# Attention layer: scores moved to the head of each head pair, attention to its tail

## Chip, cores and metric

The program runs on one core of one Trainium2 chip. The metric is device time in microseconds (us), the median of several runs of the whole program. All times of instructions come from one profiled execution.

## The reference

A conditioned transformer layer on x of 16 batches x 256 tokens x 256 features, float32, with 16 heads of 64, and 8 experts:

```python
shift = silu(t) @ W_ada.T + b_ada
h = _ln(x, ln1_g, ln1_b) + shift
qkv = (h @ Wqkv.T).reshape(b, n, 3, H, HD)
q = _ln(q, qn_g, qn_b); k = _ln(k, kn_g, kn_b)           # per head
attn = softmax(einsum('bhnd,bhmd->bhnm', q, k) / sqrt(HD))
x = x + (attn @ v).reshape(...) @ Wout.T
gate = softmax(tok @ Wgate.T); top_k per expert (512 tokens each)
tok += w * (gelu(_ln(tok[idx]) @ fc1.T + b1) @ fc2.T + b2)   # scattered back
```

## The kernel before

Stage 1 (to about 890 us) is the attention half and the gate products; stages 2 and 3 are the routing and the experts. Only stage 1 is touched.

Stage 1 is a software pipeline over batches `b` (-1 to 16; a hardware loop for 2 to 13, the rest written out) and, in a batch, over 8 **pairs** of heads, `hp` 0 to 7, unit `u = 8b + hp`. Every engine has a function `batch` that walks the pairs in the same order, each with its own instruction stream, executed strictly in the order written; semaphores (`need`) join the streams. In pair `u`:

- TensorE (PE) transposes the probabilities of unit u-2 into `mx` (L1634) and the normalised q and k of unit u+1 into `pq` (L1643); makes the scores of unit u into `sc` (`scores`, L1590); multiplies the transposed probabilities of u-2 with V into `av` (L1689, the "attention"); and does one or two **chunks** of the q, k, v projection into a bank of `ch` (`chunk`, lines L508 to L510, two chunks of 6 matmuls in pairs 7, 0, 1, 3, 4, 5). In pair 2 the output projection of pairs 4 to 7 of the batch before takes the chunks' place, in pair 6 that of pairs 0 to 3, with transposes of `tok` and the gate products (L1705). At the end of pair 1 the next batch's input rows are transposed (`xh`, L1607).
- ScalarE (ACT) brings q out of `pq` (L1186), the chunks out of `ch` (`raw` and `sq`, or `V`), makes `qk_hi` (L1152), the four exponentials (L1170, in two halves of two, `exponentials(u, hp, 0)` and `(u, hp, TT)`), and `o_hi` from `av` (L1224). In pairs 1 and 5 it starts the square-root iteration for the norms (`power_guess`, L1094 and L1096).
- VectorE (DVE) copies `mx` to `probT` (L1419), brings k out (L1427), sums squares (L1360), makes `var` (L1373, L1376), takes the row extremum `m` of the scores (L1470), `o_lo` from `av` and `o_hi` (L1479), the reciprocals (L1398).
- GpSimd (POOL) normalises the probabilities of u-1 (L1059), in pairs 1 and 5 refines the reciprocal roots (`refine`, L1018 to L1028) and scales a quarter of q/k (L965), and at the end of every pair makes `qk_lo` of unit u+1 (L1076).

Large products are exact-split: `_hi` and `_lo` operands in fp32r, three matmuls each. Transposes, attention and gate products are plain f32. The shape of a matmul in the array differs too: the scores use half its rows (64 x 128, two side by side), the attention half its columns (128 x 64, two side by side), all others the whole of it (128 x 128).

Scores of unit u wait for two counters:

```python
need(lo_ready, u + 1)     # qk_lo of this unit, from POOL in pair u-1
need(prob_ready, u)       # exponentials of unit u-1 have read sc
```

In the order of before, PE goes: `mx`, `pq`, first chunk, attention, scores, second chunk.

Of the kernel before, what the change touches and what calls it, by code (L numbers as in the profile page):

```python
# [80 lines left out]
def make_counts():  # L81
# [8 lines left out]
    for b in range(-1, B + 1):  # L90
        cur, nxt, prv = 0 <= b < B, b + 1 < B, 1 <= b <= B
        for hp, pos, name, who in batch_slots(b):
            key = (hp, pos)
            hit("slot", b, key)
            hit(who, b, key)
            if name == "gate":
                slots[-1] = (b, (6, 0), who, key)
            else:
                slots.append((b, key, who, key))
            if name in ("q", "k"):  # L100
                hit("chunk", b, key)
# [93 lines left out]
def build(nc, x, condT, w_adaT, vecs, w_qk, w_vT, w_outT, w_gateT, experts, b2s, consts, out):  # L195
    ctx = ExitStack()
    with ctx:
# [887 lines left out]
        def _(act):  # L1085
# [58 lines left out]
            def batch(b, cur, nxt, prv):  # L1144
# [15 lines left out]
                def exponentials(u, hp, first):  # L1160
# [11 lines left out]
                    if first > 0:  # L1172
                        ins.then_inc(prob_ready, 1)

                for hp in range(UNITS):
                    u = b * UNITS + hp
                    par = (hp + 1) % 2
                    ahead = (cur and nxt) or (cur and hp < UNITS - 1) or (nxt and hp == UNITS - 1)
                    live = (hp, 0) in CHUNKS and (cur if hp < 2 else nxt)
                    if ahead:  # L1180

                        need(qk_transposed, u + 2)
                        need(lo_ready, u)
                        if entry:
                            need(q_vec_ready, 1)
                        nc.scalar.activation(qkT[par][:, 0:N], pq[:, 0:N], ACT.Identity,  # L1186
                                             bias=q_vec[:, 1:2], scale=q_vec[:, 0:1]).then_inc(q_evacuated, 1)
# [28 lines left out]
                    if tail and hp == UNITS - 1:  # L1216
                        exponentials(u, hp, 0)
                    if (cur and hp > 1) or (hp < 2 and prv):
                        need(attended, u - 1)
                        if hp == 2 and prv:  # L1220
                            need(slot_filled, through("slot", b - 1, (6, 2)))
                        if hp == 6 and prv:
                            need(slot_filled, through("slot", b, (2, 0)))
                        nc.scalar.activation(o_hi[:, (hp - 2) % UNITS, :], av[:, 0:N], ACT.Copy).then_inc(o_hi_ready, 1)  # L1224
                    if live and values:
                        chunk(b, hp, 0)
# [4 lines left out]
                    if hp == 5 and nxt and not entry:  # L1231
                        power_guess(b, 4)
                    if live and values:
                        chunk(b, hp, 1)
                    if cur and not (tail and hp == UNITS - 1):
                        exponentials(u, hp, 0)
                    if cur:
                        exponentials(u, hp, TT)
                    if tail and hp == 5:
                        power_guess(b, 4)  # L1240
# [6 lines left out]
        def _(dve):  # L1247
# [155 lines left out]
            def batch(b, cur, nxt, prv):  # L1403
                last_entry = isinstance(b, int) and b == B
                entry = isinstance(b, int) and b < 0
                for hp in range(UNITS):
                    u = b * UNITS + hp
                    if entry and hp == 2:
                        silu_of_condition()
# [63 lines left out]
                    if hp == 2 and nxt and not entry:  # L1473
                        split_rows(b)
                    if (cur and hp > 1) or (hp < 2 and prv):

                        need(o_hi_ready, u - 1)
                        pair = (hp - 2) % UNITS
                        nc.vector.tensor_tensor(o_lo[:, pair, :], av[:, 0:N], o_hi[:, pair, :].bitcast(F32), ALU.subtract).then_inc(o_split, 1)  # L1479
                    if hp in (0, 3, 4, 7) and (cur if hp < 2 else nxt):  # L1480
# [29 lines left out]
                    if isinstance(b, int) and b == 0 and hp == 0:  # L1510
                        split_wout(2)

            per = 5
# [13 lines left out]
        def _(pe):  # L1527
# [75 lines left out]
            def transposed(bank, rows):  # L1603
# [4 lines left out]
                ins.then_inc(slot_filled, 1)  # L1608

            def batch(b, cur, nxt, prv):  # L1610
                drain = isinstance(b, int) and b == B
                for hp in range(UNITS):
# [23 lines left out]
                    if ahead:  # L1636
# [29 lines left out]
                    if hp == 6 and cur:  # L1666
# [4 lines left out]
                        project(first, (0, 1), False)  # L1671
                    filled = nxt or hp < 3
                    if cur and not filled:
                        scores(u, hp % 2)
                    if behind:

                        need(probT_ready, u - 1)
                        if drain:
                            need(probT_other_ready, hp + 1)
                        need(o_split, u - 2)  # L1680
                        i = (hp - 2) % GU
                        gpar = ((hp - 2) // GU) % 2
                        if i == 0:

                            need(act_read, through("act", b, (1, 1)) if hp == 6 else through("act", b, (0, 0)) - 1)
                        for jt in range(TT):
                            for hh in range(2):
                                at = (hh * TT + jt) * N
                                ins = nc.tensor.matmul(av[hh * HD:(hh + 1) * HD, 0:N], V[gpar][:, jt, i * P + hh * HD:i * P + (hh + 1) * HD],  # L1689
                                                       probT[:, at:at + N], start=(jt == 0), stop=(jt == TT - 1))  # L1690
                        ins.then_inc(attended, 1)
                    if cur and filled:
                        scores(u, hp % 2)
                    if live:
                        chunk(b, hp, 1)
                    if hp == 1 and nxt:
                        bank = take_bank(b, (1, 2))
                        need(xh_ready, b + 2)
                        transposed(bank, xh)
                    if hp == 6 and prv:  # L1700
                        bank = ch[slot_bank(b, (6, 1))]
# [5 lines left out]
                        ins.then_inc(slot_filled, 1)  # L1707
                    if hp == 2 and prv:
                        need(o_split, u - 2)
                        project(second, (7,) if drain else (6, 7), True)  # L1710
                    if hp == 6 and cur:
                        need(o_split, u - 2)
                        project(first, (2, 3), True)

# [48 lines left out]
```

## Time and profile before

| | us |
|---|---|
| median of 3 runs | 1157.24 (1156.55 to 1157.64) |
| time of the profiled execution | 1159.4 |
| its span, first to last instruction | 1157.6 |
| TensorE matmul busy | 1101.2 (95%) |
| VectorE busy | 899.9 (78%) |
| ScalarE busy | 731.6 (63%) |
| GpSimd busy | 607.3 (52%) |

Busy time of matmuls overlaps (they are pipelined), so the starts of successive groups say more than the busy column. One batch of the loop lasts 53.5 us. Times below are from the start of the span; a merged line gives the start of its first instruction, the time to the end of its last, and their count; in brackets the idle time before and what ended it.

### The profile page before, as it was taken

To read this page: it belongs to the slowest core of one execution; us is meant where nothing else is said; L and a number is where in the kernel's file an instruction comes from. 1 tells how busy PE (TensorE), PEld (TensorE's weight loads), DVE (VectorE), ACT (ScalarE), POOL (GpSimd) and SP (SyncE) were. 2 spreads that over 40 slices of the span, in tenths; PEclk is the share of its full clock that TensorE was granted. 3 is DMA by queue.
4 is the path that set the end of the run, shared out by engine and by line. 5 is a ranking of instruction groups with operands and counts; after the bars stand their busy time and mean duration, and the time that the engine had idled before them with its cause. 6 is when DMAs were issued, how large, how long until landed. Compare 5 with 4: busy or idle time off the path is not lost.

```text
span 1157.6 us, 24504 instructions
## 1 busy us (share of the span) xinstructions
PE 1101.2 (95%) x8046; PEld 860.9 (74%) x8052; DVE 899.9 (78%) x1693; ACT 731.6 (63%) x1991; POOL 607.3 (52%) x529
## 2 busy tenths in 40 slices
PE   8899999999999999999999999999988779999996
PEld 6667777777777777777777777777765248889985
DVE  6897888878887878788787878787776867777773
ACT  5667777776767677777777676777773214455441
POOL 2556555666666556656565665656562023554332
PEclk9899999999999999999999999999999998999999
DMA  5000000000000000000000000000002404554422
GB/s 184 17 10 19 20 20 19 18 18 18 18 18 20 27 25 18 18 18 18 18 18 18 18 18 18 30 15 20 10 19 84 132 18 132 168 134 119 109 29 28
DMA packets 31776, 48.62 MB, mean 42 GB/s; under 512 B 7921, under 2 KB 28529, under 8 KB 30449
## 3 DMA queue, kind: packets, MB, share of 16 engines
q1 hardware_dynamic: 25584, 39.49, 10.5%
q0 software_dynamic: 6144, 8.52, 4.0%
q8 instruction: 28, 0.46, 0.2%
q14 instruction: 20, 0.16, 0.0%
HBM read 35.29 MB, written 12.71 MB: 41 GB/s over the span
## 4 chain that ended last, share of the span: by engine, by line
issue 31%; PE 31%; POOL 21%; DVE 8%; ACT 6%; POOLq 1%; DMA 1%; SPq 0%; ACTq 0%; DVEq 0%
POOL qk_lo L1076 9%; POOL prob L1059 5%; PE ch L508 5%; PE ch L510 4%; PE ch L509 4%; POOL qn L965 3%; PE av L1689 3%; DVE m L1470 2%; PE sc L1590 2%; ACT prob L1170 2%; ACT raw L1125 1%; PE sc L508 1%; PE sc L510 1%; PE sc L509 1%; PE pq L1643 1%
## 5 line engine op out<-in xcount | busy, mean ns | idle before, releaser
L1059 POOL TENSOR_TENSOR prob<-prob,inverse 128x1024 f32<-128x1024 f32 x127 | 241.1, 1899 | 265.4 <-DVE inverse L1398 265.4
L1170 ACT ACTIVATE prob<-sc,m 128x256 f32<-128x256 f32 x512 | 235.9, 475 | 121.3 <-DVE m L1470 118.2
L1470 DVE TENSOR_REDUCE m<-sc 128x4 f32<-128x1024 f32 x127 | 155.4, 1224 | 69.9 <-PE sc L1590 69.7
L1419 DVE COPY probT<-mx 128x1024 f32<-128x1024 f32 (+1 forms) x128 | 155.2, 1212 | 59.2 <-PE mx L1634 58.1
L1076 POOL TENSOR_TENSOR qk_lo<-qkT,qk_hi 128x512 fp32r<-128x512 f32 x128 | 171.5, 1340 | 26.0 <-ACT qk_hi L1152 24.5
L508 PE MATMUL ch<-w_hi,hT_lo 128*128 128x512 f32 x384 | 170.1, 443 | 2.6 <-DVE hT_lo L1332 2.2
L509 PE MATMUL ch<-w_lo,hT_hi 128*128 128x512 f32 x384 | 152.3, 397 | 0.0
L510 PE MATMUL ch<-w_hi,hT_hi 128*128 128x512 f32 x384 | 152.0, 396 | 0.0
L1689 PE MATMUL av<-probT,V 128*64 128x256 f32 x1024 | 139.6, 394 | 8.3 <-DVE probT L1419 3.8
L1634 PE MATMUL mx<-con,prob 128*128 128x128 f32 x1024 | 134.5, 274 | 9.1 <-POOL prob L1059 7.8
L1634 PEld LDWEIGHTS mx<-con,prob 128*128 128x128 f32 x1024 | 116.0, 140 | 29.0 <-POOL prob L1059 11.7
L1689 PEld LDWEIGHTS av<-probT,V 128*64 128x64 f32 x1024 | 62.4, 136 | 69.0 <-DVE probT L1419 38.0
L1170 ACT ACTIVATION_READ_ACCUMULATOR prob<-sc,m 128x1 f32 x512 | 105.4, 206 | 0.0
L612 POOL DMA_INDIRECT out<-yout,index x32 | 52.3, 1634 | 99.9 <-DVE yout L958 93.5
L673 ACT ACTIVATE yT<-ch,b_sb 128x512 f32<-128x512 f32 x62 | 42.7, 689 | 88.5 <-PE ch L510 87.4
L1360 DVE TENSOR_REDUCE ssum<-sq 128x8 f32<-128x512 f32 x128 | 86.7, 678 | 13.2 <-ACT sq L1127 13.1
L1125 ACT ACTIVATE raw<-ch 128x512 f32<-128x512 f32 x128 | 78.0, 609 | 30.0 <-PE ch L510 30.0
L508 PEld LDWEIGHTS ch<-w_hi,hT_lo 128*128 128x128 f32 x384 | 72.3, 188 | 26.8 <-issue 2.2
L1590 PE MATMUL sc<-qk_hi,qk_lo 64*128 64x256 f32 x512 | 85.7, 330 | 1.9 <-ACT prob L1170 1.4
L1590 PEld LDWEIGHTS sc<-qk_hi,qk_lo 64*128 64x128 f32 x512 | 48.3, 184 | 50.5 <-issue 48.8
L510 PEld LDWEIGHTS ch<-w_hi,hT_hi 128*128 128x128 f32 x384 | 72.3, 188 | 17.7
L1186 ACT ACTIVATE qkT<-pq,q_vec 128x256 f32<-128x256 f32 x128 | 73.6, 575 | 18.5 <-PE pq L1643 18.4
(222 smaller groups left out, 2686.9 us busy)
## 6 DMA issues: line engine op xcount, KB each, us to landing
fcw<-experts SPq DMA_DIRECT2D x8, 2048.0 KB, 9.0
x_sb<-x SPq DMA_DIRECT2D x16, 256.0 KB, 2.7
xr_sb<-x SPq DMA_DIRECT2D x16, 256.0 KB, 2.8
out<-tok SPq DMA_DIRECT2D x16, 256.0 KB, 2.2
rows_dram<-xh SPq DMA_DIRECT2D x16, 256.0 KB, 2.2
prob<-w_qk SPq DMA_DIRECT2D x2, 512.0 KB, 6.5
qn<-w_qk SPq DMA_DIRECT2D x2, 512.0 KB, 7.2
V<-w_vT SPq DMA_DIRECT2D x2, 512.0 KB, 7.3
```

What stands on the lines that cost most here:

```text
L508: nc.tensor.matmul(psum, l_lo, r_hi, start=first, stop=False)
L509: nc.tensor.matmul(psum, l_hi, r_lo, start=False, stop=False)
L510: return nc.tensor.matmul(psum, l_hi, r_hi, start=False, stop=last)
L1059: nc.gpsimd.tensor_tensor(pr, pr, r, ALU.mult).then_inc(normalised, 1)
L1076: nc.gpsimd.tensor_tensor(qk_lo[par][:, :], qkT[par][:, :], qk_hi[par][:, :].bitcast(F32), ALU.subtract).then_inc(lo_ready, 1)
L1125: nc.scalar.activation(raw[:, c, :], bank[:, :], ACT.Copy)
L1170: ins = nc.scalar.activation(prob[hp % 2][:, g * N:(g + 1) * N], sc[:, g * N:(g + 1) * N], ACT.Exp, bias=m[hp % 2][:, g:g + 1], scale=-1.0 ...
L1419: nc.vector.tensor_copy(probT[:, 0:half], mx[:, 0:half]).then_inc(probT_ready, 1)
L1470: nc.vector.tensor_reduce(m[hp % 2][:, :], sc[:, :].rearrange("p (g n) -> p g n", n=N), AX.X, ALU.min).then_inc(max_ready, 1)
L1590: ins = nc.tensor.matmul(sc[:, at:at + N], q_part[par][rows, it * P:(it + 1) * P], k_part[par][rows, N:2 * N], start=(q_part is qk_lo), st ...
L1634: ins = nc.tensor.transpose(mx[:, to:to + P], pr[:, at:at + P], ident)
L1689: ins = nc.tensor.matmul(av[hh * HD:(hh + 1) * HD, 0:N], V[gpar][:, jt, i * P + hh * HD:i * P + (hh + 1) * HD], probT[:, at:at + N], start ...
```

## The change

In pairs with scores, `cur and (nxt or hp < 3)`, that is all pairs of batches 0 to 14 and pairs 0 to 2 of batch 15, the PE order becomes: `mx`, `pq`, (in pair 2 the transposes of `xh`, which leave pair 1), **scores**, first chunk, second chunk (in pair 2 both halves of the output projection; in pair 6 the transposes of `tok`, both halves, then the gate products), **attention**. ACT takes `o_hi` from between the chunks' reading and `qk_hi` to between the two halves of the exponentials, and with it, in pairs 1 and 5, the two readings of `V` (one ahead of and one behind the second half). DVE takes `o_lo` to the end of its pair. The counting of filled slots follows the new PE order. No instruction is added or taken away.

```diff
@@ make_counts
+        for hp, pos, name, who in sorted(batch_slots(b), key=lambda s: (s[0], 3 if s[2] == "gate" else s[1])):
+            hit("slot", b, (hp, pos))
         for hp, pos, name, who in batch_slots(b):
             key = (hp, pos)
-            hit("slot", b, key)
             hit(who, b, key)
@@ ACT, pair hp
+                    behind = (cur and hp > 1) or (hp < 2 and prv)
+                    under = cur and (nxt or hp < 3)
...
-                    if (cur and hp > 1) or (hp < 2 and prv):
-                        need(attended, u - 1)
...
-                        nc.scalar.activation(o_hi[:, (hp - 2) % UNITS, :], av[:, 0:N], ACT.Copy).then_inc(o_hi_ready, 1)
-                    if live and values:
+                    if behind and not under:
+                        attended_high(hp, u)
+                    if live and values and not under:
                         chunk(b, hp, 0)
                     if ahead and not (tail and hp > 1):
                         split_high(u, par)
...
                     if cur and not (tail and hp == UNITS - 1):
                         exponentials(u, hp, 0)
+                    if behind and under:
+                        attended_high(hp, u)
+                    if live and values and under:
+                        chunk(b, hp, 0)
                     if cur:
                         exponentials(u, hp, TT)
+                    if live and values and under:
+                        chunk(b, hp, 1)
@@ DVE, end of pair hp
+                    if behind and under:
+                        attended_low(hp, u)
@@ PE, pair hp
                         ins.then_inc(qk_transposed, 1)
+                    if hp == 2 and nxt and cur:
+                        bank = take_bank(b, (1, 2))
+                        need(xh_ready, b + 2)
+                        transposed(bank, xh)
+                    filled = nxt or hp < 3
+                    if cur and filled:
+                        scores(u, hp % 2)
                     if live:
                         chunk(b, hp, 0)
...
-                    if cur and filled:
-                        scores(u, hp % 2)
+                    if behind and not filled:
+                        attend(b, hp, u, drain)
                     if live:
                         chunk(b, hp, 1)
-                    if hp == 1 and nxt:
+                    if hp == 1 and nxt and not cur:
...
+                    if hp == 2 and prv:
+                        need(o_split, u - 2)
+                        project(second, (7,) if drain else (6, 7), True)
+                    if hp == 6 and cur:
+                        need(o_split, u - 2)
+                        project(first, (2, 3), True)
                     if hp == 6 and prv:
                         bank = ch[slot_bank(b, (6, 1))]
...
+                    if behind and filled:
+                        attend(b, hp, u, drain)
```

## Rows read from the trace of the kernel before

**Rows 1.** Page, part 4: shares of the chain of work that ended last.
```profile
issue 31%; PE 31%; POOL 21%; DVE 8%; ACT 6%; POOLq 1%; DMA 1%; SPq 0%; ACTq 0%; DVEq 0%
```

**Rows 2.** Windows, one batch, pair 7 to pair 6: length, busy time (xcount), clock, DMA.
```profile
core 0: us, PE busy (x) PEld busy (x) DVE busy (x) ACT busy (x) POOL busy (x), PEclk, DMA share, GB/s
505.16:558.70 53.54, 52.70 (x394) 40.85 (x393) 43.36 (x75) 38.57 (x116) 32.05 (x29) 1.00 0.07 20
```

**Rows 3.** Timeline, PE, pair 1: start, us, engine, line, operation, out<-in, shapes, count.
```profile
518.21 1.04 PE L1634 MATMUL mx<-con,prob 128*128 128x128 f32 x8
519.08 0.60 PE L1643 MATMUL pq<-con,qn 128*128 128x128 f32 x4
519.44 0.48 PE L508 MATMUL ch<-w_hi,hT_lo 128*128 128x512 f32 x1
...
521.01 1.08 PE L1689 MATMUL av<-probT,V 128*64 128x256 f32 x8
522.03 0.39 PE L1590 MATMUL sc<-qk_hi,qk_lo 64*128 64x256 f32 x2
...
522.93 0.51 PE L508 MATMUL ch<-w_hi,hT_lo 128*128 128x512 f32 x1
523.28 0.39 PE L509 MATMUL ch<-w_lo,hT_hi 128*128 128x512 f32 x1
...
524.44 0.60 PE L1607 MATMUL ch<-con,xh 128*128 128x128 f32 x4
524.87 1.04 PE L1634 MATMUL mx<-con,prob 128*128 128x128 f32 x8
```

**Rows 4.** Timeline, PE, first transposes of pairs 3 and 6.
```profile
531.41 1.09 PE L1634 MATMUL mx<-con,prob 128*128 128x128 f32 x8
...
551.11 1.03 PE L1634 MATMUL mx<-con,prob 128*128 128x128 f32 x8
```

**Rows 5.** Timeline, PE, last batch, end of pair 6 and start of pair 7.
```profile
870.09 1.08 PE L1689 MATMUL av<-probT,V 128*64 128x256 f32 x8
871.11 1.06 PE L1705 MATMUL ch<-wg_sb,tokT 128*128 128x8 f32 x8
...
873.54 1.04 PE L1634 MATMUL mx<-con,prob 128*128 128x128 f32 x8
874.51 0.39 PE L1590 MATMUL sc<-qk_hi,qk_lo 64*128 64x256 f32 x2
```

**Rows 6.** Timeline, ACT, pair 1.
```profile
522.14 0.39 ACT L1224 ACTIVATE o_hi<-av 128x256 fp32r<-128x256 f32 x1 [0.71 <-PE av L1689]
522.43 0.59 ACT L1130 ACTIVATE V<-ch 128x512 f32<-128x512 f32 x1
...
523.42 0.23 ACT L1094 ACTIVATE log_var<-var 128x36 f32<-128x36 f32 x1
```

**Rows 7.** Timeline, ACT, last batch, third exponential to the end of the fourth.
```profile
857.50 0.47 ACT L1170 ACTIVATE prob<-sc,m 128x256 f32<-128x256 f32 x1
...
858.31 0.21 ACT L1170 ACTIVATION_READ_ACCUMULATOR prob<-sc,m 128x1 f32 x1
```

**Rows 8.** Timeline, PE, last batch, the scores that waited for those exponentials.
```profile
858.67 0.39 PE L1590 MATMUL sc<-qk_hi,qk_lo 64*128 64x256 f32 x2 [0.72 <-ACT prob L1170]
```

**Rows 9.** Timeline, POOL, pair 1 and pair 5 (the last rows reach into pair 6).
```profile
520.67 1.90 POOL L1059 TENSOR_TENSOR prob<-prob,inverse 128x1024 f32<-128x1024 f32 x1 [2.44 <-DVE inverse L1398]
...
526.50 1.28 POOL L1076 TENSOR_TENSOR qk_lo<-qkT,qk_hi 128x512 fp32r<-128x512 f32 x1
...
547.80 1.89 POOL L1059 TENSOR_TENSOR prob<-prob,inverse 128x1024 f32<-128x1024 f32 x1 [3.15 <-DVE inverse L1398]
550.68 0.25 POOL L1018 TENSOR_TENSOR na<-guess 128x36 f32<-128x36 f32 x1 [0.98 <-ACT guess L1096]
...
553.42 1.28 POOL L1076 TENSOR_TENSOR qk_lo<-qkT,qk_hi 128x512 fp32r<-128x512 f32 x1
```

**Rows 10.** Timeline, DVE, pair 5.
```profile
548.66 1.06 DVE L1373 TENSOR_SCALAR var<-mv 128x4 f32<-128x4 f32 x1
```

**Rows 11.** Timeline, ACT, pair 5.
```profile
550.10 0.23 ACT L1094 ACTIVATE log_var<-var 128x36 f32<-128x36 f32 x1
```

More of the change, by code:

```diff
@@ L1173, in exponentials, with attended_high @@
                         ins.then_inc(prob_ready, 1)
+                def attended_high(hp, u):
+                    need(attended, u - 1)
+                    if hp == 2 and prv:
+                        need(slot_filled, through("slot", b - 1, (6, 2)))
+                    if hp == 6 and prv:
+                        need(slot_filled, through("slot", b, (2, 0)))
+                    nc.scalar.activation(o_hi[:, (hp - 2) % UNITS, :], av[:, 0:N], ACT.Copy).then_inc(o_hi_ready, 1)
                 for hp in range(UNITS):
@@ L1217, in batch @@
                         exponentials(u, hp, 0)
-                    if (cur and hp > 1) or (hp < 2 and prv):
-                        need(attended, u - 1)
[L1220 to L1223, printed above, removed]
-                        nc.scalar.activation(o_hi[:, (hp - 2) % UNITS, :], av[:, 0:N], ACT.Copy).then_inc(o_hi_ready, 1)
-                    if live and values:
+                    if behind and not under:
+                        attended_high(hp, u)
+                    if live and values and not under:
                         chunk(b, hp, 0)
@@ L1232, in batch @@
                         power_guess(b, 4)
-                    if live and values:
+                    if live and values and not under:
                         chunk(b, hp, 1)
@@ L1405, in batch, with attended_low @@
                 entry = isinstance(b, int) and b < 0
+                def attended_low(hp, u):
+                    need(o_hi_ready, u - 1)
+                    pair = (hp - 2) % UNITS
+                    nc.vector.tensor_tensor(o_lo[:, pair, :], av[:, 0:N], o_hi[:, pair, :].bitcast(F32), ALU.subtract).then_inc(o_split, 1)
                 for hp in range(UNITS):
                     u = b * UNITS + hp
+                    behind = (cur and hp > 1) or (hp < 2 and prv)
+                    under = cur and (nxt or hp < 3)
                     if entry and hp == 2:
@@ L1474, in batch @@
                         split_rows(b)
[L1475 to L1479, printed above, removed]
+                    if behind and not under:
+                        attended_low(hp, u)
                     if hp in (0, 3, 4, 7) and (cur if hp < 2 else nxt):
@@ L1511, in batch @@
                         split_wout(2)
+                    if behind and under:
+                        attended_low(hp, u)
             per = 5
@@ L1608, in transposed, with attend @@
                 ins.then_inc(slot_filled, 1)
+            def attend(b, hp, u, drain):
+                need(probT_ready, u - 1)
+                if drain:
+                    need(probT_other_ready, hp + 1)
+                need(o_split, u - 2)
+                i = (hp - 2) % GU
+                gpar = ((hp - 2) // GU) % 2
+                if i == 0:
+                    need(act_read, through("act", b, (1, 1)) if hp == 6 else through("act", b, (0, 0)) - 1)
+                for jt in range(TT):
+                    for hh in range(2):
+                        at = (hh * TT + jt) * N
+                        ins = nc.tensor.matmul(av[hh * HD:(hh + 1) * HD, 0:N], V[gpar][:, jt, i * P + hh * HD:i * P + (hh + 1) * HD],
+                                               probT[:, at:at + N], start=(jt == 0), stop=(jt == TT - 1))
+                ins.then_inc(attended, 1)
             def batch(b, cur, nxt, prv):
@@ L1671, in batch @@
                         project(first, (0, 1), False)
-                    filled = nxt or hp < 3
                     if cur and not filled:
                         scores(u, hp % 2)
[L1675 to L1691, printed above, removed]
-                    if cur and filled:
-                        scores(u, hp % 2)
+                    if behind and not filled:
+                        attend(b, hp, u, drain)
                     if live:
                         chunk(b, hp, 1)
-                    if hp == 1 and nxt:
+                    if hp == 1 and nxt and not cur:
                         bank = take_bank(b, (1, 2))
@@ L1699, in batch @@
                         transposed(bank, xh)
+                    if hp == 2 and prv:
+                        need(o_split, u - 2)
+                        project(second, (7,) if drain else (6, 7), True)
+                    if hp == 6 and cur:
+                        need(o_split, u - 2)
+                        project(first, (2, 3), True)
                     if hp == 6 and prv:
@@ L1707, in batch @@
                         ins.then_inc(slot_filled, 1)
[L1708 to L1713, printed above, removed]
+                    if behind and filled:
+                        attend(b, hp, u, drain)
             over_batches(pe, batch)
```

## The prediction, made before the changed kernel ran

> **What bounds the kernel now.** I read the chain of waits first, then the busy windows of one batch, then PE's timeline pair by pair, then the other engines' timelines around one place in pairs 1 and 5. The chain [rows 1] gives most of the span to PE and to its issue, a fifth to POOL. One batch, cut at the first transposes of pair 7, lasts 53.54 us with PE busy for 52.70 at a granted clock of 1.00 (2.4 GHz) [rows 2]: in stage 1 PE is nearly always at work, and the clock has nothing to lose or win there. So the change is worth what it does to the starts of PE's groups: the edges between them, and the waits in front of them.
>
> A plain pair, by starts in pair 1 [rows 3]: `mx` 0.87, `pq` 0.36, first chunk 1.57, attention 1.02, scores 0.90, second chunk 1.51, together 6.23 up to 524.44; the transposes of `xh` add 0.43. No wait is in it. The waits of the batch come out by subtraction: pairs 7 and 0 take 518.21 - 505.16 = 13.05 against 2 x 6.23 = 12.46, so 0.59; pairs 3 to 5 take 551.11 - 531.41 = 19.70 against 18.69, so 1.01 [rows 2 to 4]. Pair 2 takes 6.54, and streams as many columns as a plain pair; I give it a wait of 0.2. Together **1.8 us of waiting per batch**, which a better order could remove: mostly `mx` behind POOL's normalising and attention behind the copy of `mx`.
>
> **Part 1, edges on PE.** Joining f32 to f32 work saves only if a change of type costs something. Transposes (f32) to chunk (fp32r): 519.08 to 519.44 is 0.36 for four transposes that cost 0.109 each in `mx` (0.87 / 8), so the chunk starts 0.08 early and its first matmul is late by as much: no cost. Chunk back to transposes: five matmuls from 523.28 to 524.44 are 0.232 each up to the transposes, again none [rows 3]. What does cost is a change of shape. Scores (64 rows) to chunk (128 x 128), both fp32r: the first matmul takes 0.35 (522.93 to 523.28) and not 0.23 [rows 3]. Whole array to scores: in the last batch eight transposes take 0.97 up to the scores, and not 0.87, so 0.10 [rows 5]. Attention to whole array, f32 to f32: 1.02, as long as attention to scores [rows 3, 5], so its tail is no cheaper for meeting its own type.
>
> The new order has one shape change more: whole to scores, scores to whole, whole to attention, attention to whole, where before attention and scores stood together. In starts: `mx` 0.89 (0.02 for the load behind attention, an estimate below the 0.10 edges), `pq` 0.44, edge 0.10, scores 0.90, first chunk 1.51 (it now has the place of 522.93 to 524.44), second chunk 6 x 0.232 + 0.10 = 1.49, attention 1.02: **6.35, or +0.12 a pair**, +0.96 a batch (pairs 2 and 6 have the same edges). Bounds: 0 if the loads hide, 0.3 if the new edges cost as much as scores to chunk does in all. The two rules of the Trainium skill differ here: TensorE: Matmul & The Clock Gate (Step-by-step: what each phase is for) has weight loads pulled ahead of running matmuls, and by that alone the order would cost nothing and the sum be 14 us lower; TensorEngine Tiling (Array Packing) (Key Properties) says a change of tiling mode drains the engine, which speaks against this change. The 0.10 edges agree with the second.
>
> **Part 2, waits that go.** The normalised probabilities and `probT` get more time: POOL's normalising, undelayed in pair 1, ends 2.46 + 1.90 = 4.36 us into the pair [rows 3, 9], and `mx` of it comes at the next pair's start, 6.35; attention comes 5.3 us into its pair, the `probT` copy over 3 us before that. I take all 1.8 away (at the least 1.0). DVE's `o_lo` at the pair's end is due in the next attention but one group later; the projections that read it in pairs 2 and 6 come over 3 us into the pair. No cost, and nothing waits behind it but the next `probT` copy, which needs `mx` anyway (0.87 in).
>
> **Part 3, scores behind the exponentials.** Scores now want to start 0.89 + 0.44 + 0.10 = 1.43 into the pair, where they were at 3.82 [rows 3]. ACT has `o_hi` between its two halves of exponentials, and ACT's queue is in order: the second half waits for the attention, now PE's last group. From the start of attention: `o_hi` at +1.13 (521.01 to 522.14), 0.28 to the next instruction [rows 3, 6], two exponentials 858.31 + 0.21 - 857.50 = 1.02 [rows 7], 0.15 to the scores (858.52 to 858.67) [rows 7, 8]: +2.58, while PE gets from attention to the scores in 1.02 + 1.43 = 2.45. **Wait 0.12 a pair**, for six pairs 0.72 a batch. It is a loop through ACT and PE and no later pair wins it back. Bounds: 0, and 0.4 if ACT itself comes late to `o_hi`.
>
> **Part 4, scores behind `qk_lo`.** In pairs 1 and 5 POOL has refine and scaling ahead of `qk_lo`, and that starts from `var`. In pair 5 the little `var` operation lasts 1.06 us and ends at 549.72 with POOL's normalising (547.80 + 1.89 = 549.69) [rows 9, 10]: it does not run beside it. With no delay of `mx`, normalising ends 4.36 into the pair, as in pair 1 [rows 9]; so the logarithm on ACT starts about 4.55. From there to the end of `qk_lo` it was 553.42 + 1.28 - 550.10 = 4.60 in pair 5, and 526.50 + 1.28 - 523.42 = 4.36 in pair 1 [rows 6, 9, 11]; nothing in it is changed. So `qk_lo` ends 9.15 after pair 5 begins. The pair is 6.47 long, the semaphore takes 0.1 (estimate, under the 0.15 above), so the scores of pair 6 start 2.78 in: **wait 1.35**. For pair 2: 4.5 + 4.36 - 6.47 + 0.1 = 2.5 in, where `xh` brings the wish to 1.43 + 0.44 = 1.87: **wait 0.6**. Before, scores came late enough to cover this; nothing covers it now. In the other pairs POOL makes `qk_lo` straight behind `qk_hi`, long ahead. Bounds: by ACT alone (V's 0.48 between, 522.43 to the next) pair 6 waits at least 0.6, pair 2 at least 0.16; above, 1.8 and 1.0 if POOL is a little later than that.
>
> **Sum.** Per batch +0.96 - 1.80 + 0.72 + 0.60 + 1.35 = **+1.83 us**. Batches 1 to 14 have it whole; batch 0 (no attention in pairs 0 and 1) and the three pairs of batch 15 count as one more: 15 x 1.83 = 27 us. Stages 2 and 3 have nothing of it. The profiled execution, 1159.4, becomes 1186; it stands 2.2 us over the median of the runs, so the median becomes **1184 us**.
>
> **Rivals.**
> A, POOL is in time (chance 0.15): `qk_lo` ends sooner because the logarithm starts as soon as it may and POOL runs freer. Then only ACT holds the scores, 0.72 + 0.16 + 0.60 a batch: 0.96 - 1.80 + 1.48 = +0.64, 15 x = 10 us, 1167. For it: ACT is free earlier in pair 5 than before. Against: the five steps on POOL are the same.
> B, faster (0.11): neither counter is late, the scores go straight behind the transposes. 0.96 - 1.80 = -0.84 a batch, 1144. It decides at `qk_lo` of pair 5 ending under 1.4 into pair 6, 1.3 sooner than I find, and all waits together under 0.84 a batch. For it: DVE starts the row extremum 2.4 us earlier, so ACT's exponentials can too. Against: ACT's order, which ties the second half to attention.
> C, ACT comes late (0.14): first half of the exponentials, behind the chunk's reading and `qk_hi`, is not done when attention is. By my count they end together, without reserve; 0.2 late in six pairs is 1.2 a batch more, 18 us: 1202.
> D, loads hide (0.05): edges cost nothing, +0.87 a batch, 1170. The rows of part 1 are against it.
>
> **How the numbers follow.** Forecast 0.55, 1184, by itself 1174 to 1195. The range reaches to A and D below and C above: 1163 to 1205. A measurement of this kernel tells 0.2%, about 2.3 us, from no change. Faster is B, 0.11; the same needs a mean between B and A, 0.05; slower 0.84.
>
> **What would show it.** In the new trace: scores of pair 6 idle over 1 us with `qk_lo` as releaser, of pair 2 about half of that; 0.1 or so in the other pairs behind the exponentials; no wait of attention for `probT`; first matmul of the scores and of the first chunk slow, second chunk's not; `o_hi` as the last thing ahead of the second half of the exponentials, ACT idle before it in pairs 2 and 6. A batch of 55.4 us. I am wrong if the batch is under 53.5, if the scores of pair 6 start under 2 us into the pair, or if transposes behind attention start 0.1 sooner than the gate products did.

## The result and the profile after

The changed kernel takes **1197.96 us** (median; 1197.0 to 1199.42) against 1156.89 measured beside it: ratio 1.0357 [1.034, 1.0373]. It is slower, as forecast, within the range, 14 us over the point. First come the page's busy times and its chain of work, to be compared with [rows 1], then the window of one batch, pair 7 to pair 6, with the columns of [rows 2].

```profile
PE 1112.4 (93%) x8046; PEld 868.6 (73%) x8052; DVE 897.2 (75%) x1693; ACT 734.6 (61%) x1991; POOL 605.4 (51%) x529
...
PE 36%; issue 31%; POOL 21%; DVE 5%; ACT 4%; DMA 1%; POOLq 1%; SPq 1%; ACTq 0%; DVEq 0%
```

```profile
531.78:587.69 55.91, 53.29 (x395) 41.20 (x393) 43.06 (x75) 38.73 (x115) 31.94 (x29) 1.00 0.06 19
```

The same matmuls now take 55.91 us and not 53.54 [rows 2], at the same clock. The part of the batch in which PE is not busy grew from 0.84 to 2.62 us. This is a plain pair, pair 1, to be compared with [rows 3]:

```profile
488.86 1.09 PE L1673 MATMUL mx<-con,prob 128*128 128x128 f32 x8
489.79 0.60 PE L1682 MATMUL pq<-con,qn 128*128 128x128 f32 x4
490.50 0.39 PE L1611 MATMUL sc<-qk_hi,qk_lo 64*128 64x256 f32 x2
490.69 0.31 PE L1611 MATMUL sc<-qk_lo,qk_hi 64*128 64x256 f32 x2
...
491.40 0.50 PE L509 MATMUL ch<-w_hi,hT_lo 128*128 128x512 f32 x1
491.73 0.40 PE L510 MATMUL ch<-w_lo,hT_hi 128*128 128x512 f32 x1
...
492.90 0.40 PE L509 MATMUL ch<-w_hi,hT_lo 128*128 128x512 f32 x1
493.13 0.39 PE L510 MATMUL ch<-w_lo,hT_hi 128*128 128x512 f32 x1
...
494.39 1.08 PE L1645 MATMUL av<-probT,V 128*64 128x256 f32 x8
495.40 1.09 PE L1673 MATMUL mx<-con,prob 128*128 128x128 f32 x8
```

By the starts alone, `mx` takes 0.93, `pq` 0.71 with a wait at its end, the scores 0.90, the chunks 1.50 and 1.49, the attention 1.01. The scores of pairs 2, 3 and 6 (one line each) wait longer, and for POOL:

```profile
497.84 0.39 PE L1611 MATMUL sc<-qk_hi,qk_lo 64*128 64x256 f32 x2 [0.47 <-POOL qk_lo L1077]
...
505.00 0.39 PE L1611 MATMUL sc<-qk_hi,qk_lo 64*128 64x256 f32 x2 [0.65 <-POOL qk_lo L1077]
...
525.60 0.39 PE L1611 MATMUL sc<-qk_hi,qk_lo 64*128 64x256 f32 x2 [1.14 <-POOL qk_lo L1077]
```

Pairs 7, 0, 1, ... 6, from `mx` to `mx`, last 6.54, 6.47, 6.54, 7.42, 7.08, 6.47, 6.53, 8.85 us; before the change they lasted 6.76, 6.29, 6.67, 6.54, 6.83, 6.44, 6.44, 7.63 (the transposes of `xh`, 0.43, went from pair 1 to pair 2). By span, 39.9 us were added: 0.5 ahead of batch 0, 5.4 in its pairs 0 to 6, 4.2 from its pair 7 to pair 6 of batch 1, 30.5 in the 13 batches behind that (2.35 each), 0.9 from there to the end of stage 1; stages 2 and 3 gave 1.6 back.

### The profile page after: what moved, and what is told of

Read it like the earlier page. It is cut to its first block, busy times and chain, and to the rows that moved or that the text cites. A ratio compares the mean times of both kernels' runs of the same rounds, so it can differ in the third digit from the quotient of the medians.

```text
span 1197.5 us, 24532 instructions
## 1 busy us (share of the span) xinstructions
PE 1112.4 (93%) x8046; PEld 868.6 (73%) x8052; DVE 897.2 (75%) x1693; ACT 734.6 (61%) x1991; POOL 605.4 (51%) x529
## 4 chain that ended last, share of the span: by engine, by line
PE 36%; issue 31%; POOL 21%; DVE 5%; ACT 4%; DMA 1%; POOLq 1%; SPq 1%; ACTq 0%; DVEq 0%
POOL qk_lo L1077 9%; PE ch L509 6%; PE ch L511 5%; PE ch L510 5%; POOL prob L1060 5%; PE sc L1611 3%; POOL qn L966 3%; PE mx L1673 3%; PE av L1645 2%; PE sc L509 1%; PE sc L510 1%; PE sc L511 1%; DVE hit L846 1%; ACT sq L1128 1%; PE pq L1682 1%
## 5 line engine op out<-in xcount | busy, mean ns | idle before, releaser
L1171 ACT ACTIVATE prob<-sc,m 128x256 f32<-128x256 f32 x512 | 238.8, 479 | 62.6 <-DVE m L1492 55.5
L509 PE MATMUL ch<-w_hi,hT_lo 128*128 128x512 f32 x384 | 163.9, 427 | 0.8 <-DVE hT_lo L1345 0.8
L1673 PEld LDWEIGHTS mx<-con,prob 128*128 128x128 f32 x1024 | 109.8, 141 | 52.5 <-issue 45.0
L1673 PE MATMUL mx<-con,prob 128*128 128x128 f32 x1024 | 139.8, 279 | 3.5 <-POOL prob L1060 3.4
L1424 DVE TENSOR_TENSOR o_lo<-av,o_hi 128x256 fp32r<-128x256 f32 x128 | 54.1, 423 | 88.0 <-ACT o_hi L1183 85.4
L1611 PEld LDWEIGHTS sc<-qk_hi,qk_lo 64*128 64x128 f32 x512 | 52.9, 185 | 74.7 <-POOL qk_lo L1077 46.9
L509 PEld LDWEIGHTS ch<-w_hi,hT_lo 128*128 128x128 f32 x384 | 73.3, 191 | 27.4 <-DVE hT_lo L1345 1.0
```

Of the source, the lines that this page charges most:

```text
L509: nc.tensor.matmul(psum, l_lo, r_hi, start=first, stop=False)
L1171: ins = nc.scalar.activation(prob[hp % 2][:, g * N:(g + 1) * N], sc[:, g * N:(g + 1) * N], ACT.Exp, bias=m[hp % 2][:, g:g + 1], scale=-1.0 ...
L1611: ins = nc.tensor.matmul(sc[:, at:at + N], q_part[par][rows, it * P:(it + 1) * P], k_part[par][rows, N:2 * N], start=(q_part is qk_lo), st ...
L1673: ins = nc.tensor.transpose(mx[:, to:to + P], pr[:, at:at + P], ident)
```

## The experiments

All started from the changed kernel and kept its arithmetic. The pair's lengths below are from `mx` to `mx` in the steady loop, "+2.87" is a start counted from the pair's `mx`.

**e1: scores back between the chunks**, attention at the tail.

```diff
@@ PE, pair hp
-                    if cur and filled:          # behind pq and xh
-                        scores(u, hp % 2)
                     if live:
                         chunk(b, hp, 0)
...
-                    if cur and not filled:
+                    if cur:                     # between the chunks
                         scores(u, hp % 2)
```

> The changed kernel with one thing moved: scores stand between the two chunks (in pairs 2 and 6 between the two halves of the output projection), attention stays at the tail. Theory (the loss is waits in front of the scores, for qk_lo in pairs 2, 3 and 6 and for the exponentials elsewhere, plus 0.12 us a pair of shape changes): the scores start 2.9 us or later into the pair, all these waits go, the four shape changes stay; a plain pair 6.35, a batch 52.7 to 53.0 us, 1142 to 1148 in all, under the kernel before. Rival (attention at the tail is what costs, through the late o_hi and o_lo): a batch stays above 55, 1185 to 1198.

Measured 1173.19 us, ratio 1.0127 [1.0103, 1.0151]. Plain pairs are all 6.39 with the scores at +2.87: their waits are gone. But pair 2 grew to 7.63 and pair 6 is still 8.50, for a wait that neither the prediction nor the expectation names: the output projection waits for a bank that ACT frees too late, with its second reading of `V`, which the change had moved behind the exponentials. First the line of the table of waits (us in total, times, longest), then the row of pair 6:

```profile
PE ch L509 <- ACT V L1131: 15.5, 29, 0.9
```

```profile
454.74 0.38 PE L509 MATMUL ch<-wo_hi,o_lo 128*128 128x256 f32 x1 [0.56 <-ACT V L1131]
```

Some 25 of the 41 us hang on the place of the scores. The time expected, 1142 to 1148, was missed by 25; the bank is 11 of these (e5).

**e2: scores at the tail**, directly ahead of the attention.

```diff
@@ PE, pair hp
-                    if cur and filled:          # behind pq and xh
-                        scores(u, hp % 2)
...
+                    if cur and filled:          # behind both chunks
+                        scores(u, hp % 2)
                     if behind and filled:
                         attend(b, hp, u, drain)
```

> Scores moved further, directly ahead of the attention at the tail, so that the two narrow shapes stand together again. Theory: one shape change less than with scores between the chunks; a plain pair 6.23, a batch 51.8 us, 1127 to 1133 in all. Rival (shape changes are hidden by loads pulled ahead, and only waits count): the same as with the scores between the chunks, within 3 us. Second rival (row extremum and exponentials now come too late and hold POOL's normalising and the transposes): slower than with scores between the chunks.

Measured 1329.77, ratio 1.1477 [1.1449, 1.1505]; pairs of 7.54 to 9.36. The theory fell. Its second rival was right that the row extremum and the exponentials come too late, but not in what they hold: the transposes are not delayed. In the plain pairs it is the second chunk that waits, 1.1 us, as ACT's readings of the chunks stand behind the exponentials. From the table of waits:

```profile
ACT prob L1171 <- DVE m L1492: 361.9, 124, 5.2
...
PE ch L509 <- ACT sq L1128: 71.2, 62, 2.7
```

**e3: attention back between the chunks**, scores early.

```diff
@@ PE, pair hp
-                    if behind and not filled:   # between the chunks
+                    if behind:
                         attend(b, hp, u, drain)
...
-                    if behind and filled:       # at the tail
-                        attend(b, hp, u, drain)
```

> Scores stay directly behind the transposes, attention goes back between the chunks. Theory: the loop attention, o_hi, second half of the exponentials, next scores is cut, so the 0.13 us in front of the scores of plain pairs goes and a plain pair is 6.35; the waits for qk_lo in pairs 2, 3 and 6 stay or grow a little, as POOL's work counts from the start of its pair. A batch 55.0 to 55.4, 1183 to 1190 in all. Rival (qk_lo alone is the cost): 1197 to 1199, unchanged. Rival (joining attention to the transposes did save something on PE): slower than 1198.

Measured 1195.88, ratio 1.0327 [1.0304, 1.0351]. The loop through ACT is gone: in pair 0 the scores come at +1.45, where in the changed kernel they come at +1.56.

```profile
422.85 1.09 PE L1673 MATMUL mx<-con,prob 128*128 128x128 f32 x8
423.77 0.60 PE L1682 MATMUL pq<-con,qn 128*128 128x128 f32 x4
424.30 0.39 PE L1611 MATMUL sc<-qk_hi,qk_lo 64*128 64x256 f32 x2
```

The pair is 6.47 all the same: now both chunks stand behind another shape, and each has a slow first matmul, where in the changed kernel the transposes behind the attention lose 0.06 in all (0.93 against 0.87; in e3 they take 0.87 in pairs 1 to 6, though 0.92 in the pair shown). Attention ahead of the transposes is the cheaper place, by about the 0.1 that the loop costs. The range expected was missed by 6 us.

**e4: POOL makes `qk_lo` first** in pairs 1 and 5, ahead of refinement and scaling.

```diff
@@ POOL, pair hp
+                    early = hp in (1, 5) and cur and nxt
+                    if early:
+                        ...                     # qk_lo of unit u + 1
                     if hp == 1 and cur:
                         refine(b, 0)
                         scale(b, 0, 2)
```

> The changed kernel with one thing moved on POOL: in pairs 1 and 5 qk_lo is made ahead of the refining and scaling, not behind it. Theory: the scores of pair 6 then wait only for the exponentials behind V (0.6 us in place of 1.23), those of pair 2 0.16 in place of 0.57; the wait in pair 3, whose qk_lo stands behind pair 2's scaling, grows by about 0.4 because pair 2 gets shorter: 0.6 us less a batch, 1186 to 1191 in all. Rival (the order on ACT alone sets these starts): no change, 1197 to 1199.

Measured 1192.02, ratio 1.0297 [1.0273, 1.0321], 1 us over the range expected; the batch is 55.30, which is 0.63 less against 0.6 expected. In pair 6 the scores come at +2.04 instead of +2.67 and then wait for ACT, the lower bound of part 4 (0.6); pair 2 gains 0.4, and pair 3 gives 0.4 back. The scores of pair 3, then of pair 6:

```profile
445.52 0.39 PE L1616 MATMUL sc<-qk_hi,qk_lo 64*128 64x256 f32 x2 [0.94 <-POOL qk_lo L1082]
...
465.49 0.39 PE L1616 MATMUL sc<-qk_hi,qk_lo 64*128 64x256 f32 x2 [0.51 <-ACT prob L1176]
```

**e6: e4, and POOL does its second scaling in pairs 1 and 5** too, so that nothing stands ahead of `qk_lo` in pairs 2 and 6.

```diff
@@ POOL, pair hp
                         scale(b, 0, 2)
+                        scale(b, 0, 3)          # the same in pair 5
-                    if hp == 2 and cur:
-                        scale(b, 0, 3)
```

> The changed kernel with POOL reordered: in pairs 1 and 5 qk_lo first, then refining and both of POOL's scalings, so that no scaling stands ahead of qk_lo in any pair. Theory (POOL's order is the largest term, also in pair 3, which the prediction gave 0.12 only): the waits for qk_lo go in pairs 2, 3 and 6, what is left there is the exponentials' (0.1 to 0.2 in pairs 2 and 3, 0.6 in pair 6): 1.5 us less a batch than the changed kernel, 1172 to 1180 in all. Rival (pair 3 waits for something else, DVE's long pair 2): pair 3 stays near 7.1 us, 1185 to 1192. Second rival (POOL's normalising in pairs 2 and 6 is pushed back and holds the transposes): 1190 or more.

Measured 1185.81, ratio 1.0239 [1.0222, 1.0256], 6 us over the range expected and inside that of the first rival; the batch is 54.70. Pair 3 falls from 7.08 in the changed kernel, and 7.47 in e4, to 6.85. Its scores come at +1.63, as in the plain pairs: the scaling ahead of `qk_lo` was their wait, and not, as the rival had it, DVE's long pair 2. What pair 3 still has over pair 4 (6.48) lies mostly behind its scores: 1.70 and 1.60 for the two chunks against 1.51 and 1.49.

**e5: e1 with both readings of `V` ahead of the second exponentials.**

```diff
@@ ACT, pair hp
                     if live and values and under:
                         chunk(b, hp, 0)
+                        chunk(b, hp, 1)
                     if cur:
                         exponentials(u, hp, TT)
-                    if live and values and under:
-                        chunk(b, hp, 1)
```

> Scores between the chunks as in the first experiment, and on ACT in pairs 1 and 5 both readings of V ahead of the second half of the exponentials. There the projection of pairs 2 and 6 waited 0.7 us for the bank that the second reading frees. Theory: these two waits go and nothing else moves, plain pairs stay 6.39 (edges 0.16 over the kernel before), a batch 53.0 in place of 54.4: 1150 to 1156 in all, about the time of the kernel before or a little under. Rival (the later exponentials hold the scores or POOL's normalising in pairs 2 and 6): 1165 to 1175.

Measured 1162.01 against 1158.72, ratio 1.0034 [1.0022, 1.0047], 6 us over the range expected. The bank's waits are gone, and pairs 2 and 6 fall to 6.88 and 7.68; but pair 3 now is 6.80 and pair 7 is 6.90, not 6.39.

**e7: scores and attention both at the tail, ACT reordered**: chunks read in their own pair, `o_hi`, `V`, all exponentials last; DVE's `o_lo` behind the extremum, its split of the hidden rows ahead of it.

```diff
@@ ACT, pair hp
-                    if cur and not (tail and hp == UNITS - 1):
-                        exponentials(u, hp, 0)
                     if behind and under:
                         attended_high(hp, u)
                     if live and values and under:
                         chunk(b, hp, 0)
+                        chunk(b, hp, 1)
+                    if cur and not (tail and hp == UNITS - 1):
+                        exponentials(u, hp, 0)
                     if cur:
                         exponentials(u, hp, TT)
-                    if live and values and under:
-                        chunk(b, hp, 1)
...
```

> Scores and attention together at the tail as in the second experiment, and ACT's order made for it: qk_hi, then both chunks read in their own pair, o_hi, V, and the exponentials last; DVE has o_lo behind the row extremum again and the split of the rows ahead of it. Theory (in the second experiment the chunks' banks waited for readings that stood behind late exponentials; on PE the order itself is the cheapest, one shape change less than in the changed kernel and no wait of attention for probT): a plain pair 6.2 to 6.3, a batch 51.6 to 52.4 us, 1126 to 1140 in all, under the kernel before. Rival (scores at the tail leave too little time from scores over row extremum and exponentials to the next pair whatever ACT does first): over 1160.

Measured 1226.56, ratio 1.0593 [1.0563, 1.0624]: the theory fell, the rival was right. Pairs 0 and 1, free of waits, last 6.18 to 6.19, against 6.38 to 6.39 with the scores between the chunks: setting the scores apart from the attention costs 0.20 a pair (`mx` to `mx`, pair 0, in e7 and in e1):

```profile
436.10 1.09 PE L1669 MATMUL mx<-con,prob 128*128 128x128 f32 x8
...
442.28 0.44 PE L1669 MATMUL mx<-con,prob 128*128 128x128 f32 x2
```

```profile
412.64 1.09 PE L1673 MATMUL mx<-con,prob 128*128 128x128 f32 x8
...
419.02 0.66 PE L1673 MATMUL mx<-con,prob 128*128 128x128 f32 x4
```

But pairs 2, 3, 6 and 7 take 7.6 to 8.8. In pair 3 `mx` waits for POOL's normalising and `pq` for POOL's scaling, and the second chunk waits 1.69 for DVE:

```profile
456.20 1.09 PE L1669 MATMUL mx<-con,prob 128*128 128x128 f32 x8 [0.97 <-POOL prob L1060]
457.73 0.65 PE L1678 MATMUL pq<-con,qn 128*128 128x128 f32 x4 [0.44 <-POOL qn L966]
```

**e8: e5 with DVE's staging of input rows moved** from pair 6 to the end of pair 7.

```diff
@@ DVE, pair hp
-                    if hp == 6 and has_second(b):
+                    if hp == 7 and has_second(b):    # and behind probT
                         ...
                         input_rows(rstd[0])
```

> The arrangement of e5 (scores between the two chunks, attention at the tail, ScalarE's two readings of V's bank ahead of the second half of the exponentials), with one move more: VectorE's staging of the input rows goes from pair 6 to the end of pair 7, behind its transposes of the probabilities. In e5 pair 7 is 6.89 us and not 6.4, its attention waiting 0.5 for those transposes. If the staging stood in front of them, pair 7 goes back to about 6.4, the batch from 53.8 to about 53.3, and the whole to about 1154 (15 x 0.5 = 7 less than e5's 1162), just faster than before. Rival: what is staged later makes the input transposes of the next batch's first pair late instead, pair 0 grows by what pair 7 gives back, and the time stays at 1162.

Measured 1158.52, ratio 1.001 [1.0, 1.002]. Pair 7 went to 6.39 and the batch to 53.3, as said, 0.25 less than before the change; the whole, expected at 1154, is no faster than before, since batch 0 lost what the others won.

**e9: e8 with POOL's order of e6.**

```diff
@@ POOL, pair hp
+                    early = hp in (1, 5) and cur and nxt
...
+                        scale(b, 0, 3)
```

> e8 with GpSimd's order of e6 as well (qk_lo ahead of the refinement in pairs 1 and 5, both scalings on GpSimd's side there). In e5 pair 3 is 6.80 us against 6.39 of the plain pairs. If it waits for the scaling, it goes to 6.4 to 6.6 and the batch to 52.9 to 53.1, the whole to 1148 to 1151, some 0.7 per cent faster than before. Rival: pair 3 waits for VectorE's split of the hidden rows instead; then GpSimd's order changes nothing, or moves 0.2 to 0.4 into pairs 2 and 6, and the time is e8's within 3 us.

Measured 1163.63, ratio 1.0045 [1.0029, 1.006]. The rival was right in its cause, and the time is 5 us worse than e8's: pair 3 grew from 6.80 to 7.03. Its `pq` no longer waits for the scaling, but its chunk waits for DVE's low split of the hidden rows, which took 1.65 beside POOL's `qk_lo` (in e8 1.42):

```profile
431.10 0.47 PE L509 MATMUL ch<-w_hi,hT_lo 128*128 128x512 f32 x1 [0.40 <-DVE hT_lo L1347]
```

**e10: e8 with DVE's split of the output weights behind the row extremum** in batch 0.

```diff
@@ DVE, pair hp
-                    if isinstance(b, int) and b == 0 and hp > 2:
-                        split_wout(hp)
                     if cur:
                         ...                     # row extremum m
+                    if isinstance(b, int) and b == 0 and hp > 2:
+                        split_wout(hp)
```

> e8 with one move in batch 0 alone: VectorE's split of the output weights, which stands ahead of the row extremum in pairs 3 to 7, goes behind it. In e8 batch 0 loses 2.4 to 3 us against the kernel before, all in pairs 4 to 7, where the extremum begins 1 to 3 us after the scores and the exponentials wait for it. If the split in front of it is the cause, the four pairs go back to 6.4 to 7.7 us, batch 0 gains 2.5 to 5, the steady batches stay at 53.3, and the whole comes to 1153.5 to 1156, 0.1 to 0.4 per cent faster than before. Rival: the low half of the attention's output and the copy of the transposed probabilities, which then stand behind the split, become late in its place; batch 0 and the time stay as in e8.

Measured **1153.47** (1151.43 to 1154.93) against 1157.52, ratio 0.9962 [0.9947, 0.9977]: faster than the kernel before by 0.4%. Against e8, pairs 4 to 7 of batch 0 fell from 7.71, 7.94, 8.10, 7.98 to 6.39, 6.39, 6.83, 6.58; the steady batch stayed at 53.3.

**e11: e10 with DVE's inverse ahead of its scaling** in pair 2.

```diff
@@ DVE
-                    rows_first = (hp == 2 and prv) or (hp in (6, 7) and nxt)
+                    rows_first = hp in (6, 7) and nxt
```

> e10 with VectorE's inverse of the row sums ahead of its share of the scaling in pair 2 (in e8 the inverse ends at 423.4 and GpSimd's normalising waits 2.27 for it). Then GpSimd's own scaling comes 1.2 us earlier and the wait of 0.21 of pair 3's transposes for it goes. If that is all that holds pair 3, it falls from 6.80 to 6.6 and the time by 3 us against e10. Rival: the low split of the hidden rows, done at 427.1, holds the chunk at 427.25 whatever the transposes do; then pair 3 stays within 0.1 of 6.80 and the time within 2 us of e10.

Measured 1165.82, ratio 1.008 [1.006, 1.01]. Neither theory held: pair 3 grew to 7.53. POOL's normalising did come earlier, and now ran beside DVE's two scalings, which took 3.23 us and not 1.28, with extremum and hidden rows late behind them (DVE, then POOL):

```profile
421.61 3.23 DVE L966 TENSOR_TENSOR qn<-raw,rstd 128x512 f32<-128x512 f32 x2
...
425.89 0.41 DVE L1343 CAST hT_hi<-hT 128x512 fp32r<-128x512 f32 x1
426.34 0.69 DVE L1344 TENSOR_TENSOR hT_lo<-hT,hT_hi 128x512 fp32r<-128x512 f32 x1
```

```profile
420.94 1.90 POOL L1060 TENSOR_TENSOR prob<-prob,inverse 128x1024 f32<-128x1024 f32 x1 [0.15 <-DVE inverse L1410]
422.80 1.49 POOL L966 TENSOR_TENSOR qn<-raw,rstd 128x512 f32<-128x512 f32 x1
```

**e12: the changed kernel with e10's move alone** (the diff is e10's).

> The changed kernel with e10's move alone: in batch 0 VectorE's split of the output weights goes behind the row extremum in pairs 3 to 7. Batch 0 costs 5 us more after the change than before, where the sum had about 2, and 2.5 of the 5 lie in pair 7 (9.93 us against 7.46), whose scores wait 1.89 for the exponentials and which ends at the lower clock. If the extremum behind the split makes the exponentials late, pair 7 falls to 7.6 to 8.1, the clock stays up there, and the whole goes to 1195.5 to 1196.5, ratio about 1.034; the steady batches stay at 55.93. Rival: the scores of pair 7 are late with V's readings on ScalarE; then pair 7 stays near 9.9 and the time at 1198.

Measured 1196.29, ratio 1.0328 [1.031, 1.0346], as expected. Pair 7 of batch 0 lasts 7.42 instead of 9.93, its scores wait 0.31 for POOL, and the clock is 1.00 there. Stage 1 ends 3.9 us earlier than in the changed kernel, the whole only 1.7: stages 2 and 3, the same in both, took 268.8 us in e12's profiled execution and 266.6 in the changed kernel's.

## Why the prediction was right, and where 14 us came from

The sign, the mechanism and most terms held; the batch cost +2.37 and not +1.83. One term of the batch failed, the wait of pair 3, and so did the sum's treatment of the first batches.

- **Edges**, +0.96: held. The scores of pair 0 come at +1.45 without the loop (e3), and with 0.90, 1.50, 1.49 and 1.01 the free pair is 6.35, as worked out (by e3's pair 4, with 0.56 from `pq` to the scores, 6.39). Joining f32 to f32 gave nothing: attention to transposes takes 1.01, attention to gate products took 1.02 [rows 5], and the `mx` behind the attention takes 0.93, not 0.87 (the sum had 0.89). First matmuls are slow where the shape changes, scores 0.19 and first chunk 0.33, while the second chunk's takes 0.23. This is what the Trainium skill, TensorEngine Tiling (Array Packing) (Key Properties), says of a change of tiling mode, that the engine drains. That hidden loads make the edges free, rival D, is out. e7 against e1 prices the separated scores by themselves: 0.20 a pair.
- **Waits that go**, -1.80: by subtraction 2.37 - 0.96 - 3.24 (the waits below) = -1.83. In the whole trace the matmuls of the attention waited 3.8 us for `probT` before and 1.2 after, their weight loads 38.0 and 1.9 (table of waits, before, then after):

```profile
PEld av L1689 <- DVE probT L1419: 38.0, 74, 1.2
```

```profile
PEld av L1645 <- DVE probT L1441: 1.9, 3, 1.0
```

- **Behind the exponentials**, 0.12 a pair: 0.11 in pairs 0 and 4, 0.17 to 0.19 in 7, 1 and 5 (starts of the scores less 1.45), 0.76 in five pairs against 0.60. In all five the last exponential ends 0.14 ahead of the scores. C is out: `o_hi` comes 1.13 to 1.21 behind the start of the attention, and 1.13 was counted. A and B are out by the next term.
- **Behind `qk_lo`**, pairs 2 and 6: 0.60 and 1.35 predicted, 0.53 (2.44 less 1.45 and about 0.46 for `xh`) and 1.22 (2.67 less 1.45) measured. The steps are there as counted; ACT's logarithm begins at 520.97, 4.56 into pair 5 (4.55 said), and `qk_lo` ends 4.58 behind it (4.60 said). ACT, then POOL, pair 5:

```profile
520.97 0.23 ACT L1095 ACTIVATE log_var<-var 128x36 f32<-128x36 f32 x1 [0.93 <-DVE var L1389]
```

```profile
518.93 1.90 POOL L1060 TENSOR_TENSOR prob<-prob,inverse 128x1024 f32<-128x1024 f32 x1 [1.79 <-DVE inverse L1411]
521.54 0.25 POOL L1019 TENSOR_TENSOR na<-guess 128x36 f32<-128x36 f32 x1 [0.72 <-ACT guess L1097]
...
523.28 1.04 POOL L966 TENSOR_TENSOR qn<-raw,rstd 128x512 f32<-128x512 f32 x1 [0.16 <-POOL rstd L1029]
524.28 1.27 POOL L1077 TENSOR_TENSOR qk_lo<-qkT,qk_hi 128x512 fp32r<-128x512 f32 x1
```

- **The step that failed**: "In the other pairs POOL makes `qk_lo` straight behind `qk_hi`, long ahead." In pairs 2 and 6 POOL has its second scaling in front of it, which the description of the kernel leaves out as well: it names POOL's scaling in pairs 1 and 5 alone. In pair 2 `qk_lo` also runs beside DVE's split of the hidden rows and takes 1.72 and not 1.28. So the scores of pair 3 wait 0.73 (2.18 less 1.45), where the sum had 0.12: +0.61 a batch, and the batch missed by 0.54. Pair 6 is long enough to cover its scaling: pair 7 waits for the exponentials alone. e6 shows the cause: without that scaling in pair 2 the scores of pair 3 come at +1.63. POOL, then DVE, pair 2:

```profile
502.05 1.23 POOL L966 TENSOR_TENSOR qn<-raw,rstd 128x512 f32<-128x512 f32 x1
503.23 1.72 POOL L1077 TENSOR_TENSOR qk_lo<-qkT,qk_hi 128x512 fp32r<-128x512 f32 x1
```

```profile
501.14 1.23 DVE L1344 CAST hT_hi<-hT 128x512 fp32r<-128x512 f32 x1
502.40 1.42 DVE L1345 TENSOR_TENSOR hT_lo<-hT,hT_hi 128x512 fp32r<-128x512 f32 x1
```

- **The first batches** were taken like the others and cost more. Pair 7 of batch 0 was 2.5 us longer than before. In pairs 3 to 7 of this batch DVE has the split of the output weights ahead of the row extremum; before the change the scores came later, and those of pairs 3 to 7 did not wait. Now the scores of pair 6 begin at 76.50, but their extremum has to wait until 81.34, behind a `wo_lo` that runs beside POOL's normalising. The exponentials follow it, and the scores of pair 7 wait for them until 84.94 (DVE and POOL, pair 6, and the window of the stretch behind those scores, columns as in [rows 2]):

```profile
79.38 2.04 DVE L1300 TENSOR_TENSOR wo_lo<-wo_sb,wo_hi 128x256 fp32r<-128x256 f32 x1
81.34 1.21 DVE L1492 TENSOR_REDUCE m<-sc 128x4 f32<-128x1024 f32 x1
```

```profile
79.25 1.90 POOL L1060 TENSOR_TENSOR prob<-prob,inverse 128x1024 f32<-128x1024 f32 x1 [3.19 <-DVE inverse L1411]
```

```profile
86.70:90.10 3.40, 3.40 (x10) 2.67 (x8) 3.37 (x4) 1.66 (x4) 2.08 (x2) 0.52 0.02 5
```

PE, which had idled 1.89 us in that pair before its scores, runs this stretch at 0.52 of its clock, near the lower level of 1.2 GHz, so here the clock did have something to lose: the pair's two chunks take 4.55 and not 2.99. e12 takes the split away from there and the pair is 7.42. Most of what else batch 0 costs, 4.9 us, lies in its first four pairs and was not tried: their scores wait 1.20 for `qk_lo` in pair 0, 1.78 and 2.81 for the exponentials in pairs 1 and 3. Part of it is scatter of the clock: e12 is alike up to there, and its scores of pair 1 wait 1.77, but its clock stayed up behind them and the pair is 1.5 us shorter. The windows from the first chunk of pair 1 to the end of that pair, in the changed kernel and in e12:

```profile
38.46:42.91 4.45, 4.45 (x14) 3.44 (x13) 2.00 (x3) 3.26 (x12) 3.27 (x7) 0.62 0.01 2
```

```profile
38.47:41.37 2.90, 2.90 (x15) 2.31 (x13) 2.00 (x3) 1.72 (x5) 1.89 (x4) 1.00 0.01 3
```

So it is not shown that the split alone brought the clock down in pair 7.

By span, 39.9 came where 27.4 were said. Of the 12.5 between (the parts are rounded), 0.52 x 14 = 7.3 is the steady batches (2.35 and not 1.83), nearly all of it pair 3; 0.5 + 5.4 + 1.9 - 1.8 = 6.0 is the beginning, where 1.9 is what batch 0's pair 7 to pair 6 of batch 1 cost beyond a steady batch; the end gives 0.9 - 1.6 = -0.7.

The kernel of e10 shows how far the change could be brought: attention ahead of the transposes, the scores left between the chunks, so that neither ACT nor POOL holds them. It is 0.4% faster than before, and only after three orders on ACT and DVE were set right behind it. Whether the kernel before would gain from such moves too was not tried, so it is not shown that the 0.4% belongs to the change.

## What to carry to other kernels

When a consumer is moved early, recount the producers of every one of its operands in every variant of the loop body, not only where the trace already shows the producer late: each pair that differs by one instruction on any engine has its own due time. An order that is best for edges is worth 0.1 to 0.2 us a pair here, a single late operand 0.5 to 1.2; settle the operands first.

## What the hardware showed that was not expected

Some instructions of DVE and POOL hold each other up for most of an instruction, not in proportion. `wo_lo` took 2.04 beside POOL's normalising, ending 0.27 behind it (rows of pair 6 above); in e10, where the normalising is not beside it, it took 0.43:

```profile
61.24 0.43 DVE L1299 TENSOR_TENSOR wo_lo<-wo_sb,wo_hi 128x256 fp32r<-128x256 f32 x1
```

In the same way `hT_lo` took 1.42 beside POOL and 0.69 without it (e11), and 3.23 for two scalings in e11 stands against 1.28 in e9. Not every pair does this: the row extremum took 1.21 at 81.34, with POOL's scaling running from 81.10. The Trainium skill, SBUF — State Buffer (SBUF: two separate sides), tells of a shared pair of ports that one of the two locks for a whole instruction, among others for a DVE operation with two SBUF inputs against a POOL operation that reads SBUF. The traces agree: `wo_lo`, `hT_lo` and the scalings read two such operands, the extremum reads the scores alone. But the cast `hT_hi`, with one operand, took 1.23 beside POOL as well, and 0.41 in e11. This is also why e9 and e11, each right about the wait it removed, made the time longer: they changed which POOL instruction runs beside a DVE one.
